# Keys projected with tokens on partitions and turned one chunk pair ahead, with the first stage and some block copies reordered

## What is computed

```python
xn = layernorm(x)
q, k, v, u = split(xn @ W_qkvu.T)            # 4 x 512; 16 heads of 32
q, k = silu(q), silu(k)
# per head, in blocks: o = (q*q_decay) @ kv + ((q @ k.T) * diag_decay) @ v
#                      kv = block_decay * kv + (k*k_decay).T @ v
o = u * o * rsqrt(mean(o*o) + eps);  attn = o @ W_out.T
scores = xn @ w_router;  the best 256 tokens are chosen, in order
h = rms_norm(chosen) * ln1; 16 query and 8 key/value heads of 128, rotated
x1 = chosen + softmax(causal(q @ k.T)) @ v @ wo
processed = x1 + (silu(h2 @ w_gate) * (h2 @ w_up)) @ w_down
out = x + attn + (xn, with the chosen rows gated to processed)
```

## Time and profile before

| | us |
|---|---|
| median of 3 runs | 485.04 (484.81 to 485.53) |
| the profiled execution | 482.49 |
| its span, first to last instruction | 480.4 |
| TensorE busy | 464.9 |
| VectorE, ScalarE, GpSimd busy | 306.5, 231.1, 190.4 |

### The profile page before, as it was taken

How to read it: one execution, slowest core, us unless ns; L and a number is a source line. 1 busy time by engine, 2 the same in 40 slices (tenths; PEclk the granted TensorE clock), 3 DMA queues, 4 the chain that set the end, 5 groups by cost and what they waited for, 6 DMA issues and landing times. The chain is left out here.

```text
span 480.4 us, 11875 instructions
## 1 busy us (share of the span) xinstructions
PE 464.9 (97%) x4839; PEld 422.7 (88%) x4839; DVE 306.5 (64%) x635; ACT 231.1 (48%) x404; POOL 190.4 (40%) x179
## 2 busy tenths in 40 slices
PE   6999999999999999999999998999999999999994
PEld 6999899898998999989989877898888878999993
DVE  5798867875399999864357787877654536230221
ACT  7831242222267687321342456755766757454430
POOL 3002152121110232024169768640471442689862
PEclk9899999999999999999999999999999999999998
DMA  7965845324410211005525545664446632565403
GB/s 225 394 139 104 116 117 108 98 79 134 144 56 2 59 57 56 3 24 176 199 89 198 183 129 179 213 220 154 153 155 220 203 104 89 156 177 190 158 1 44
DMA packets 36342, 63.74 MB, mean 133 GB/s; under 512 B 5360, under 2 KB 6912, under 8 KB 36160
## 3 DMA queue, kind: packets, MB, share of 16 engines
q1 hardware_dynamic: 35744, 61.67, 42.4%
q0 software_dynamic: 544, 1.31, 1.6%
HBM read 49.84 MB, written 13.13 MB: 131 GB/s over the span
## 5 line engine op out<-in xcount | busy, mean ns | idle before, releaser
L1168 POOL TENSOR_TENSOR wlo<-raw,whi 128x512 fp32r<-128x512 f32 x96 | 125.9, 1344 | 82.5 <-ACT whi L549 82.5
L1234 PE MATMUL banks<-HTh,whi 128*128 128x256 f32 x224 | 64.9, 290 | 2.5 <-DVE rope L910 2.4
L1235 PE MATMUL banks<-HTl,whi 128*128 128x256 f32 x224 | 63.3, 283 | 0.0
L1236 PE MATMUL banks<-HTh,wlo 128*128 128x256 f32 x224 | 63.3, 283 | 0.0
L830 DVE TENSOR_TENSOR A<-banks,DEC 128x512 f32<-128x512 f32 x64 | 39.8, 684 | 30.8 <-PE banks L1292 29.6
L1147 POOL TENSOR_TENSOR state_dec<-state,small 128x128 f32<-128x128 f32 x16 | 8.5, 529 | 109.1 <-DVE state L841 109.1
L549 ACT ACTIVATE whi<-raw 128x2048 fp32r<-128x2048 f32 x24 | 45.8, 1908 | 10.1 <-PE banks L1236 10.1
L1234 PEld LDWEIGHTS banks<-HTh,whi 128*128 128x128 f32 x224 | 42.8, 191 | 3.8 <-issue 3.3
L1235 PEld LDWEIGHTS banks<-HTl,whi 128*128 128x128 f32 x224 | 42.9, 191 | 0.3
L1236 PEld LDWEIGHTS banks<-HTh,wlo 128*128 128x128 f32 x224 | 42.9, 191 | 0.0
L1274 PE MATMUL banks<-xTh,WKh 128*128 128x256 f32 x128 | 38.6, 302 | 1.6 <-DVE xTl L753 1.6
(11 more groups left out here) (237 smaller groups left out, 1304.3 us busy)
## 6 DMA issues: line engine op xcount, KB each, us to landing
X<-in_x SPq DMA_DIRECT2D x16, 256.0 KB, 6.4
xn_all<-XN SPq DMA_DIRECT2D x16, 256.0 KB, 7.2
uo_all<-uo SPq DMA_DIRECT2D x16, 256.0 KB, 2.9
raw<-in_wq SPq DMA_DIRECT2D x4, 1024.0 KB, 5.5
UR<-uo_all SPq DMA_DIRECT2D x16, 256.0 KB, 5.5
XR<-in_x SPq DMA_DIRECT2D x16, 256.0 KB, 3.4
raw<-in_wo SPq DMA_DIRECT2D x4, 1024.0 KB, 5.8
out<-XR SPq DMA_DIRECT2D x16, 256.0 KB, 2.4
```

The lines of the kernel that those rows point to most:

```text
L1168: ins = Q.tensor_tensor(low[:, k, :], raw[b % 3][:, k, :], high[:, k, :].bitcast(f32), ALU.subtract)
L1234: T.matmul(dst, lh, rh, start=first, stop=False)
L1235: T.matmul(dst, lh, rl, start=False, stop=False)
L1236: return T.matmul(dst, ll, rh, start=False, stop=last)
```

## The change

- Keys are projected in V's form, tokens on partitions, into new buffers KN (two of two chunks). TensorE then turns them (`keys_turned`, 16 times instead of 15) and a new ScalarE copy (`turned_keys`) writes them to KT. Chunks 0 and 1 are turned in slot -1, chunk N + 2 in slot N, behind the second tile and just ahead of the mean square. The first key tile runs on chunk 0's tokens as soon as they are there, with its three parts one behind the other.
- The decayed keys come from KN and are made by GpSimd behind the decayed queries, not by VectorE.
- Tiles 0 to 5 have six different banks, so they need no evacuation before.
- First stage: the decay tables go behind the query weights, V's copies ahead of the last table; VectorE makes Q's low parts before the statistics of tiles 2 and 3; the router products are taken apart and later. DEC is made triangular by 16 selects on GpSimd, and the mask tri, with its memset and select, is gone.
- Slot 15: the sum of squares and mean square of chunk 14 go behind a rotation and the third unit, with another bank.
- Attention: Q2's high copy goes into step 1; the last two heads are normalised on VectorE; U0's copies go behind the loop, and D0's load from step 17 to 19.

```diff
+        KN = [at(f"KN{p}", 112 + 4 * p, [P, CH, DM]) for p in range(2)]
         QR = [at(f"QR{i}", kb, [P, 4, SEL]) for i, kb in enumerate((112, 158, 96, 104))]
...
-        hi_after = {0: "Q2", 2: "O0", 4: "Q3", 6: "O1", 8: "O2", 9: "O3", 12: "G0", 16: "U0"}
-        load_at = {0: "Q3", 1: "O1", 3: "O2", 5: "O3", 7: "G0", 9: "U0", 10: "G1", 13: "U1", 17: "D0"}
+        hi_after = {2: "O0", 4: "Q3", 6: "O1", 8: "O2", 9: "O3", 12: "G0"}
+        load_at = {0: "Q3", 1: "O1", 3: "O2", 5: "O3", 7: "G0", 9: "U0", 10: "G1", 13: "U1", 19: "D0"}
...
+        def rms_bank(N):
+            return pick_bank if N == N_TILES - 2 else out_bank
         def sum_of(j):
...
-            return B[tile - 2] if tile in (2, 3) else B[2 + tile % 2]
+            return B[{2: 0, 3: 1, 4: 4, 5: 7}.get(tile, 2 + tile % 2)]
...
                     if name == "K":
-                        act.wait_ge(q_w_lo if g else k_w_lo, NK), act.wait_ge(s_ps, used), act.wait_ge(kt_ps, used)
+                        act.wait_ge(q_w_lo if g else k_w_lo, NK), act.wait_ge(k_dec, used), act.wait_ge(kt_ps, used)
                     if name == "Q":
                         act.wait_ge(q_w_lo, NK), act.wait_ge(s_ps, used), act.wait_ge(q_dec, used)
                     if name == "V":
                         act.wait_ge(u_w_lo if g else v_w_lo, NK), act.wait_ge(pv_ps, used), act.wait_ge(kv_ps, used)
                     if name == "U":
                         act.wait_ge(v_w_lo, NK), act.wait_ge(u_w_lo, NK), act.wait_ge(uo_ok, used)
-                if name == "V":
-                    dst = VT[g % 2][:, j, :]
+                if name in "KV":
+                    dst = {"K": KN, "V": VT}[name][g % 2][:, j, :]
                 else:
-                    dst = {"K": KT, "Q": QT, "U": UT}[name][g % 2][:, 2 * j:2 * j + 2, :].rearrange("p k m -> p (k m)")
+                    dst = {"Q": QT, "U": UT}[name][g % 2][:, 2 * j:2 * j + 2, :].rearrange("p k m -> p (k m)")
                 S.activation(dst, proj_bank(tile)[:], ACT.Silu if name in "KQ" else ACT.Copy).then_inc(proj_sb, 1)
+            def turned_keys(M):
+                act.wait_ge(kt_ps, M + 1)
+                if M >= 2 * CH:
+                    act.wait_ge(s_ps, M - 2 * CH + 1)
+                S.activation(chunk(KT, M), tiles4(turn_bank[:]), ACT.Copy).then_inc(kt_sb, 1)
...
                 act.wait_ge(rms_ps, N + 1)
-                S.activation(ms_all[:, N:N + 1], out_bank[:, 0:1], ACT.Identity, bias=eps_rms).then_inc(ms_ok, 1)
+                S.activation(ms_all[:, N:N + 1], rms_bank(N)[:, 0:1], ACT.Identity, bias=eps_rms).then_inc(ms_ok, 1)
...
                                  ACT.Exp, scale=age).then_inc(decays_ok, 1)
-                for h in (range(0, 6), range(6, 8), range(8, NH))[part]:
+                for h in (range(0, 4), range(4, 8), range(8, NH))[part]:
                     ins = S.activation(DEC[:, by_row(h), :], lag[:], ACT.Exp, scale=shead[:, h:h + 1])
...
             decay_tables(0)
-            decay_tables(1)
             first_weights_hi("K", w_raw_k, k_w_hi, (0, 1))
             xt_high(0)
             xt_high(1)
             first_weights_hi("K", w_raw_k, k_w_hi, (2, 3))
             first_weights_hi("Q", w_raw_q, q_w_hi, range(NK))
+            decay_tables(1)
+            weights_hi("V", v_w_hi)
             decay_tables(2)
...
                 count_marks(ranked(N, 0))
-                if N == -2:
-                    weights_hi("V", v_w_hi)
+                if N == -1:
+                    turned_keys(0)
                 in_position(N, 1, tiles)
-                if N >= 1:
+                if 0 <= N < N_TILES - CH:
+                    turned_keys(N + CH)
+                if 1 <= N < N_TILES - 1:
                     mean_square(N - 1)
...
                 in_position(N, 2, tiles)
+                if N == -1:
+                    turned_keys(1)
                 if N == N_TILES - 1:
+                    mean_square(N - 1)
                     block_hi(5)
...
                     split_uo(out_at[h] + 1)
+                if h == 1:
+                    block_hi(block_of["Q2"])
                 if h == FH + 1:
...
                     S.activation(PT[:, p % 2, :], B[4][:, 0:3 * P], ACT.Copy).then_inc(pt_ok, 1)
-                if h < FH:
+                if h < FH - 2:
                     normalised(h)
...
                     S.activation(OTh[:, g % 2, :], B[5][:, 0:SEL], ACT.Identity, bias=value_bias(g)).then_inc(ot_hi, 1)
+            block_hi(block_of["U0"])
             act.wait_ge(var_s_ok, 2)
...
-            def key_decayed(N):
-                dve.wait_ge(kt_ps, N + 1), dve.wait_ge(kv_ps, N)
-                V.tensor_tensor(kdec[:], turn_bank[:], KD[:], ALU.mult).then_inc(k_dec, 1)
             def new_state(N):
...
             first_weights_lo("K", k_w_hi, k_w_lo, (1, 2, 3))
+            first_weights_lo("Q", q_w_hi, q_w_lo)
             for M in range(CH, NXN):
                 ln_stats(M)
-            first_weights_lo("Q", q_w_hi, q_w_lo)
             for M in range(CH, NXN):
...
             ln_norm(NXN)
-            for M in range(1, NXN + 1):
-                router(M)
-            dve.wait_ge(decays_ok, 4), dve.wait_ge(masks_ok, 2)
-            V.tensor_tensor(DEC[:], DEC[:], tri[:].unsqueeze(1).to_broadcast([P, NH, P]), ALU.mult).then_inc(dec_ok, 1)
             for N in slots_of_chunks:
                 if N >= 0:
                     mask(N)
                 if N == -1:
                     xt_low(N + XT_AHEAD)
-                if N >= 1:
+                if 1 <= N < N_TILES - 1:
                     squares_summed(N - 1)
...
                     ln_stats(M)
-                if 0 <= N < N_TILES - 2:
-                    key_decayed(N)
                 in_position(N, 0)
                 if NXN <= N + XT_AHEAD < N_TILES:
                     turned_norm(N + XT_AHEAD)
-                if N == N_TILES - 2:
-                    key_decayed(N)
                 for M in ln_tiles(N) if N > -CH else []:
+                    router(M - NXN)
                     ln_norm(M)
-                    router(M)
+                if N == RANK - 2:
+                    for M in range(N_TILES - NXN, N_TILES):
+                        router(M)
                 if N == RANK - 1:
...
                 if N == N_TILES - 1:
+                    squares_summed(N - 1)
                     uo_low(0)
...
                     V.reciprocal(pinv[:, h % 2, :], psum_[:, h % 2, :]).then_inc(sum_ok, 1)
+                if FH - 2 <= h < FH:
+                    dve.wait_ge(sum_ok, h + 1), dve.wait_ge(pt_ps, h - 1)
+                    for t, cols in ((0, slice(0, P)), (1, slice(P, 3 * P))):
+                        ins = V.tensor_scalar(PN[:, h % 2, cols], PR[:, h % 2, cols], pinv[:, h % 2, t:t + 1], None,
+                                              ALU.mult)
+                    ins.then_inc(pn_ok, 1)
                 if h in unit_of_step:
...
+            def key_decayed(N):
+                pool.wait_ge(kv_ps, N), pool.wait_ge(proj_sb, NPROJ * (N // CH) + N % CH + 1)
+                Q.tensor_tensor(kdec[:], KN[N // CH % 2][:, N % CH, :], KD[:], ALU.mult).then_inc(k_dec, 1)
             def state_decayed(N):
...
             ln_rstd(range(CH, NXN))
+            pool.wait_ge(decays_ok, 4)
+            for n in range(NH):
+                ins = Q.affine_select(out=DEC[:, n, :], in_=DEC[:, n, :], compare_op=ALU.is_ge, fill=0.0, base=0,
+                                      pattern=[[1, P]], channel_multiplier=-1)
+            ins.then_inc(dec_ok, 1)
             for N in slots_of_chunks:
                 if ln_tiles(N):
                     ln_rstd(ln_tiles(N))
                 if N >= 0:
                     q_decayed(N)
+                if 0 <= N < N_TILES - 1:
+                    key_decayed(N)
                 if N == HIDDEN:
...
             for h in range(STEPS):
+                if h == 1:
+                    block_lo(block_of["Q2"])
                 if h in hi_after:
                     block_lo(block_of[hi_after[h]])
                 if h == 2:
                     out_rms(1)
             rows_rms(1)
-            for b in range(block_of["G1"], len(order)):
+            for b in (block_of["U0"], *range(block_of["G1"], len(order))):
                 block_lo(b)
...
                     pe.wait_ge(xt_lo, M)
+                if M == NXN - 1:
+                    pe.wait_ge(kt_sb, 1)
                 for k in range(NK):
...
                 w_split = W_SPLIT[name]
-                if i == 0:
+                if i == 0 and g:
                     pe.wait_ge(xt_lo, CH * (g + 1))
                 if g == 0 and j == 0 and name in "VU":
                     pe.wait_ge(v_w_lo if name == "V" else u_w_lo, NK)
-                if tile >= 4:
-                    pe.wait_ge(proj_sb, tile - 3 if tile < 6 else tile - 1)
+                if tile >= 6:
+                    pe.wait_ge(proj_sb, tile - 5 if tile < 8 else tile - 1)
                 bank = proj_bank(tile)
+                if tile == 1:
```

(53 more changed lines are left out.)

11 lines of the change are left out of this document (4 added, 7 removed).

## The result

The prediction was wrong, in sign as well as in size. The changed kernel takes 485.99 us (median of 20 runs, 483.61 to 489.85), the kernel before 484.67 (20 runs beside it, 483.33 to 486.07). The ratio is 1.003 (95% interval 1.0016 to 1.0044): 0.3% slower, where 479.3 and a gain of 5.7 were forecast. The profiled execution took 486.21 for a span of 484.3.

A forecast was written before the change was run, and what follows sets the result against it. The prediction took TensorE, busy 97% of the span, as the bound. Its gains, 1.5 + 1.4 + 0.8 + 0.4 + 0.3 + 0.5 + 0.7 = 5.6, called 5.7, took 485.04 to 479.3 us; range 476.9 to 482.3.

The forecast's parts named there:

- 1 first stage: Start to the scores of chunk 0: earlier first key tile, ScalarE's queue setting the end at 35.6; gain 1.5 us.
- 2, 3 key tiles and turns, slots 1 to 13: Chunk slots: fourteen wide key tiles at 0.1 each save 1.4 us; one restart fewer in thirteen slots saves 0.8.
- 4 slot 0: Chunk slot 0: score reductions moved behind the statistics shrink a 0.5 us stall; gain 0.4 (0 to 0.6).
- 5 slot 15: Slot 15: the sum of squares behind a rotation shortens a 0.65 us wait; gain 0.3 (0 to 0.65).
- 6 attention step 1: Attention step 1: Q2's block copy moved later shortens the 1.5 us rotation stall; gain 0.5 us (0 to 1.4).
- 7 end of attention: End of attention: normalising the last two heads on VectorE cuts a 1.1 us stall; gain 0.7 (0.2 to 1.1).
- 7 U0's block copies: Behind the attention loop: U0's low part fits GpSimd's 5.78 us idle gap; no cost, up to 5 without that cover.
- The fourth rival: Chunk slots: decayed keys on GpSimd come after TensorE wants them; 490 us, 5 slower; chance 0.06.
- a sign of being wrong: Chunk slots: TensorE waiting for GpSimd's decayed-key product would show the forecast wrong; no wait there was expected.
- The other two signs: First stage ending after 36.5, or last-stage blocks arriving late, would show the forecast wrong.
- The fifth rival: Waits for copies of turned keys in slots and a wait in another step give back all; 485 us; chance 0.06.
- a reason for the unlucky end: First stage: GpSimd's later variance powers stand behind the 16 DEC selects; the selects were costed at nothing.

The follow-up runs named there:

- before_again: The kernel before, unaltered, in another profiled execution: 482.09 us (one run).
- before_third: The kernel before, unaltered, in one more profiled execution: 483.38 us (one run).
- u0_moved: The kernel before with only U0's copies moved behind the attention loop and D0's load two steps later: 488.32 us, ratio 1.0057.
- attention_old: Changed kernel with U0's and D0's moves undone, four more awake matmuls, chunk 0's GpSimd products first, Q2's copies and last two normalisations as before: 478.72 us, 0.9934.
- u0_back: The changed kernel with U0's copies and D0's load back at their old places in the attention loop: 482.85 us, ratio 0.9947.
- after_again: The changed kernel once more, unaltered, beside the kernel before: 485.89 us, ratio 1.0022.
- shifted: The changed kernel with U0's and D0's moves undone and four more awake matmuls (16 for 12): 479.23 us, ratio 0.9935.
- sbc_late: The changed kernel with U0's and D0's moves undone and the 1 MB scores broadcast held until chunk 6's scores are done: 480.36 us, ratio 0.9959.

## Why the prediction was wrong, point by point

The ledger, in us, with each term's measured value. Four profiles stand for the kernel before (before, before_again, before_third, u0_moved up to the end of attention); the columns beside them are those with the change.

| step | forecast | measured | from |
|---|---|---|---|
| 1 first stage | −1.5 | −1.0 | 37.12, 35.79, 37.20, 35.87 (mean 36.5) against 34.99 to 35.63 in seven (mean 35.5) |
| 2, 3 key tiles and turns, slots 1 to 13 | −2.2 | −1.7 | 201.2 in before_again against 199.5 in decays_first |
| 4 slot 0 | −0.4 | 0 | mean 16.0 (15.50 to 16.90) against 15.9 (15.39 to 16.31); 1.2 of the 16.90 are pauses put down to issue |
| 5 slot 15 | −0.3 | −0.2 | 15.10 against 14.87 |
| 6 attention step 1 | −0.5 | 0 | −0.39, given back within two steps |
| 7 end of attention | −0.7 | −0.3 | attention_old against decays_first |
| 7 U0's block copies | 0 | +3.0 | u0_back against after_again; +3.5 in u0_moved |
| not in the sum: pause in slot 6 | 0 | +1.1 | 16.02 to 16.60 in six (mean 16.3) against 15.2 |
| sum | −5.6 | +0.9 | runs: +1.1 (after_again) and +1.3 |

**The step that failed** is the last one of part 7: "Nothing; without that cover it would cost up to 5". The cover was real for GpSimd: it sat idle, and the low part came long before TensorE wanted U0. The mistake was to ask only whether the moved work was on time, and not who worked during those 5.8 us of idleness. In them VectorE makes `delta`, and TensorE waits for it. The fourth rival had the mechanism, the two engines on the same memory, and the prediction even read it from qdec at 1.58 and 2.07, but from GpSimd's side and for the chunk slots. The dear side is VectorE's: 0.48 a product becomes 1.50. The Trainium skill (GPSIMD Engine Reference, section 1, Specifications) names two cases of contention: VectorE reading two tensors, or working in a two-port performance mode. The prediction took up only the first. `uol`, with two tensors, went from 0.69 to 1.75, as the page has it. `delta` has one tensor input and still took over three times as long, so by the page it would be the second case; no row here shows in which mode it ran. In the chunk slots the rival itself hardly came about: TensorE waits 0.2 for the decayed keys of slot 0, which the prediction named as a sign of being wrong, and behind slot 0 for neither product. The other two signs, a first stage that ends after 36.5 and blocks that arrive late, stayed away: none of the three looked at VectorE's work beside the moved copies. The fifth rival's price, 485, is near the measured time by luck; it had waits in the slots, and another cause gave the loss.

**Step 1** was right in its chain: TensorE starts at 9.61 (9.6), the first evacuation is at 23.09 (23.1), turned keys 0 end at 28.68 (28.9), scores at 35.56 (35.6). The size was off on the other side. The kernel before has two first stages. TensorE's timeline in before_again:

```profile
11.29 0.39 PE L1274 MATMUL banks<-xTh,WKh 128*128 128x256 f32 x1 [0.79 <-DVE xTl L753]
...
35.79 0.39 PE L1292 MATMUL banks<-QT,KT 32*128 32x128 f32 x4
```

and one of before_third:

```profile
11.37 0.39 PE L1274 MATMUL banks<-xTh,WKh 128*128 128x256 f32 x1 [1.69 <-DVE xTl L753]
...
37.20 0.50 PE L1292 MATMUL banks<-QT,KT 32*128 32x128 f32 x8
```

With a wait of 0.8 the granted clock stays at 1.00 and the scores start at 35.8; with 1.6 or 1.7 the mean grant over 12 to 18 is 0.72 and they start at 37.1 or 37.2. The prediction was made on an execution of the second kind, and against that one the gain is 1.56, as forecast. None of the thirteen profiles with the change shows the dip, so over both kinds the gain is 1.0.

**Steps 2 and 3.** Even slots became 0.24 shorter and odd slots 0.04 (15.40 to 15.16, 15.20 to 15.16), slot 4 only 0.04. If the odd slots show the restart alone, one restart fewer is worth 0.04, not 0.08, and two key tiles 0.2, so 0.1 for each as forecast; no run parts the two. The figure of the Trainium skill (TensorE: Matmul & The Clock Gate, section "Wait — 56ns, not 53.3ns?"), 2.5 ns a matmul and so 0.03 a tile, is too small here.

**Step 4.** The score reductions left the queue ahead of the stall, but the stall does not end with them. It ends with GpSimd's variance power, which waits for VectorE's statistics. These wait in turn for a load of tokens, 1.6 to 2.7 in eight profiles with the change (2.59 in u0_back) and 0.4 at most in the three of the kernel before; an earlier start of the slot only lengthens that wait. The prediction named that queue as "a reason for the unlucky end" and costed the gain from the other side of it. The select operations cost nothing, as said: 16 in 4.0.

**Steps 5 to 7.** Right in kind. In step 6 a rotation waits 1.05 at 297.64 where it was 1.5, and the next 0.51 at 305.02, which gives the gain back. In step 7 the wait of 1.1 became 0.3 in the changed kernel, but two of 0.4 in u0_back.

**The pause in slot 6** no view of the kernel before could show, since it comes with the new order of TensorE's instructions; by the traces it goes with an instruction transfer that comes late, behind the broadcast of the scores. Nor could the pauses of 2.4 to 2.7 in sum in slot 11: all seven profiles of the first and last group have them, and the first one of the changed kernel, but none of the eight of the second and third, nor the first one of the kernel before. The first and second group ran on one chip. They go with the medians of the kernel before (484.81 and 485.17 with them, 482.55 and 481.63 without). u0_moved has them with the kernel before's code in the slots, so they come to both kernels; that they cancel in the ratios is likely but not shown, and what decides them stays open.

**The better kernel** is decays_first: the change without U0's move, with four more awake matmuls and GpSimd's products first in slot 0. Its ratio is 0.9932 (0.9914 to 0.9950), 478.21 against 481.63, 3.4 below the kernel before. By ratio shifted (0.9935) and attention_old (0.9934) are as good; by the span of the profile decays_first is the shortest, 475.6 against 477.2 and 477.6.

## What to carry to other kernels

An idle engine is not free room. Before moving work into a gap, look at what the engine that shares its memory does there and who waits for that one; here 5 us of hidden GpSimd work beside 1 us of critical VectorE work cost 3. Profile the kernel before more than once when a wait and a clock dip stand in the stage that is to be changed: one execution may be the dear one of two kinds, and the gain read from it too large. Where a stall of under 1 us with no releaser comes and goes with the length of the code ahead of it, shift the stream by an instruction or two, look for instruction transfers beside a large data transfer, and read the trace of each trial: sbc_late's slot stayed long although its pause was gone.

## What the runs showed of the hardware

- VectorE's product of one 128x512 tensor by a column takes 0.48 alone and 1.50 beside a GpSimd difference of two tensors; its difference of two tensors 0.69 and 1.75. GpSimd loses 15% (5.05 to 5.80 for four).
- TensorE paused 0.40 to 0.95 at one place of its instruction stream in six executions of one layout, and the place moved by two records when two records were left out ahead of it. Each time a 16 KB instruction transfer ended 1.3 to 1.5 before the scores went on; with the 1 MB broadcast held back, the transfer came 3.6 earlier than in u0_back and there was no pause.
- At one place of the program, behind 1.09 us of work in a stretch of 3, TensorE was granted 0.50 in the next stretch; in another execution, behind 1.22 of 3, it was granted 1.00.
